# A deformable convolution sampled without gathers: nine taps by dense bilinear weights, on one core of Trainium2

## What is computed

```python
off_out = conv2d(x, off_w) + off_b[None, :, None, None]
o = off_out[:, :2 * DG * K].reshape(Bb, DG, K, 2, Hh, Ww)          # DG = 2 groups, K = 9 taps
mask = jax.nn.sigmoid(off_out[:, 2 * DG * K:]).reshape(Bb, DG, K, Hh, Ww)
py = o[:, :, :, 0] + iy + ky[None, None, :, None, None]
px = o[:, :, :, 1] + ix + kx[None, None, :, None, None]
g = deform_sample(x, py, px) * mask[:, :, None]                    # bilinear, zero outside
out = jnp.einsum('odck,bdckhw->bohw', wr, g)
```

## Time and profile before

| | us |
|---|---|
| three runs | 4657.04, 4685.74, 4686.9 |
| their median | 4685.74 |
| the profiled execution, whole time | 4699.3 |
| its span | 4697.5 |
| mean granted TensorE clock, as a share of 2.4 GHz | 0.774 |

### The profile page before, as it was taken

How to read it: one execution, slowest core, us unless ns; L and a number is a source line. 1 busy time by engine, 2 the same in 40 slices (tenths; PEclk the granted TensorE clock), 3 DMA queues, 4 the chain that set the end, 5 groups by cost and what they waited for, 6 DMA issues and landing times. The chain is left out here.

```text
span 4697.5 us, 54006 instructions
## 1 busy us (share of the span) xinstructions
PE 3017.8 (64%) x20519; PEld 1314.3 (28%) x20519; DVE 2951.6 (63%) x3460; ACT 2245.1 (48%) x1945; POOL 1156.9 (25%) x1229
## 2 busy tenths in 40 slices
PE   3777479999999989999999985143143114411112
PEld 2454333233333333333333332021121112211111
DVE  5999747999999967999999961033321322232222
ACT  1444226999999967999999940000000000000000
POOL 2000010000000000000000002655665665556663
PEclk7665579999999999999999987575566556655555
DMA  2200000000000000000000001112112211211111
GB/s 42 85 1 1 1 3 1 2 1 1 1 2 1 2 1 1 1 1 1 1 2 1 2 13 36 43 42 55 45 49 51 54 47 45 59 40 45 49 44 33
DMA packets 125704, 106.26 MB, mean 23 GB/s; under 512 B 100432, under 2 KB 102608, under 8 KB 125436
## 3 DMA queue, kind: packets, MB, share of 16 engines
q0 software_dynamic: 36864, 75.57, 5.7%
q1 hardware_dynamic: 86940, 26.43, 2.6%
q10 hardware_dynamic: 1632, 0.56, 0.1%
HBM read 82.50 MB, written 19.96 MB: 22 GB/s over the span
## 5 line engine op out<-in xcount | busy, mean ns | idle before, releaser
L1533 ACT ACTIVATE adder_layer_Z<-adder_layer_CP,AN 128x2048 f32 x984 | 1873.9, 2033 | 31.7 <-PE PS L1498 30.9
L1498 PE MATMUL PS<-adder_layer_Z,c_adder_out 128*32 128x512 f32 x16896 | 1843.8, 593 | 57.9 <-ACT adder_layer_Z L1533 33.6
L1579 DVE TENSOR_SCALAR adder_layer_Z<-adder_layer_CP,AW 128x2048 f32 x1128 | 1369.9, 1283 | 43.7 <-PE PS L1498 29.9
L1902 POOL DMA_INDIRECT sampler_G<-neighbours,sampler_IDX x1152 | 1096.5, 952 | 753.5 <-issue 348.3
L1498 PEld LDWEIGHTS PS<-adder_layer_Z,c_adder_out 128*32 128x32 f32 x16896 | 644.5, 110 | 1256.9 <-issue 1187.4
L2038 ACT ACTIVATE sampler_VT<-PS 128x512 f32<-128x512 f32 x64 | 38.2, 598 | 1497.0 <-remote 921.8
L2020 PE MATMUL PS<-sampler_VT,DC 128*64 128x128 f32 (+1 forms) x640 | 157.4, 414 | 897.4 <-ACTq L2041 454.0
L1954 DVE TENSOR_TENSOR sampler_G<-sampler_G,PS 128x2304 f32<-128x2304 f32 x64 | 163.5, 2554 | 840.4 <-issue 436.0
L1586 DVE SCALAR_TENSOR_TENSOR adder_layer_Z<-adder_layer_CP,AW,adder_layer_Z 128x1024 f32<-128x1024 f32 x384 | 476.4, 1282 | 35.6 <-issue 35.6
L2020 PEld LDWEIGHTS PS<-sampler_VT,DC 128*64 128x64 f32 (+1 forms) x640 | 112.9, 210 | 945.5 <-issue 476.0
L2012 PE MATMUL PS<-c_ident,sampler_VAL 128*128 128x128 f32 (+1 forms) x320 | 78.3, 401 | 386.1 <-DVEq L1960 297.3
(11 more groups left out here) (342 smaller groups left out, 2082.4 us busy)
## 6 DMA issues: line engine op xcount, KB each, us to landing
sampler_G<-neighbours,sampler_IDX POOLq DMA_INDIRECT x1152
neighbours<-top_k_zero SPq DMA_DIRECT2D x16, 578.0 KB, 7.2
neighbours<-sampler_HT SPq DMA_DIRECT2D x256, 32.0 KB, 1.7
X<-in_x SPq DMA_DIRECT2D x8, 256.0 KB, 6.2
out<-X SPq DMA_DIRECT2D x8, 256.0 KB, 3.1
P<-in_L_conv_conv_w SPq DMA_DIRECT2D x4, 144.0 KB
P<-in_L_conv_add_w SPq DMA_DIRECT2D x4, 144.0 KB
RAW<-in_L_conv_w SPq DMA_DIRECT2D x4, 144.0 KB
```

Of the source, the lines that this page charges most:

```text
L1498: mm = t.matmul(PS[32 * j:32 * j + 32, k, :], K["adder_out"][:, 32 * i:32 * i + 32], Z[:, r % SLOTS, j, c:c + BANK], start=False, stop=Fal ...
L1533: op = a.activation(z(r, j), seen(ch, ty, tx), ACT.Relu, bias=ANf[:, weight(ty, tx, j, i)])
L1579: op = v.tensor_scalar(z(r, j), seen(ch, ty, taps[0]), AWf[:, weight(ty, taps[0], j, i)], 0.0, ALU.subtract, ALU.max)
L1902: g.indirect_dma_start(G[th % RING][:, k, :], None, tables[b], bass.IndirectOffsetOnAxis(ap=IDX[:, b % 2, step, k:k + 1], axis=0))\
```

## The change

The tables in DRAM, their clearing in an earlier phase (`zero`, 16 transfers of 578 KB), the indices, the gathers and the transposes of sampled values go. In their place each bilinear sample is a dense product: with positions py and px, the value is the sum over all 32 rows y and 32 columns x of relu(1 - |py - y|) * relu(1 - |px - x|) * mask * feature(y, x). Such a function of distance is called a hat.

A quad q is one pair, one half of its pixels (512) and one tap: 4 * 2 * 9 = 72 quads. For a quad, 4 groups (2 halves of the batch by 2 channel groups) take 32 partitions each:
- `positions`: TensorE copies the four groups' py and px from `OFF` to 32 partitions each (8 products); ScalarE makes the hats in two passes (Abs, then Relu).
- `masks`: 4 products copy the mask; VectorE multiplies the x hats by it (`HXM`).
- `spread_x`: 4 products spread the x hats to 128 partitions (4 rows by 32 columns), and ScalarE copies them to `HXS`.
- for each of 8 tiles c of 4 image rows: `spread_y` spreads the y hats of the four groups by 4 products of 32 rows each, in two pairs of PSUM banks; the product with `HXS` (128 x 1024 for each pair) is made by VectorE from PSUM for 10 of the quad's 16 pairs, and for the 6 in `POOLED` by GpSimd, after a copy to SBUF by ScalarE (`move`); `contract` multiplies the features `HT` by these weights with 4 products of 32 columns each, three tiles late (`LAG`).
- ScalarE copies the quad's sums to `V`; after 9 quads `deform` multiplies by the deformable weights (9 products), and the leaky ReLU, the 1x1 convolution and the sum follow as before.

The six banks of PSUM used for spreading are three sets of two (`SETS`), given round in the order of `ring_tiles`: TensorE fills the set of tile n only when tile n - 3 has been read (`await_read`). Bank 6 takes the contraction and bank 7 the convolutions. The stages of the next pair are now halves of 512 pixels, 12 of them, and `background` sets one product of them after each tile c: 100 products in 144 places a pair. SyncE loads five constant tables, and writes the output in halves.

```diff
-TP = H + 2
-NENT = TP * TP
 TILES = PX // 128
-STEPS = TILES * HALVES
-GK = DG * TAPS
+GROUPS4 = HALVES * DG
+QUADS = 2 * NB * TAPS
+SETS = 3
+LAG = 3
+NW = 8
+NE = 3
+POOLED = ((0, 1), (2, 0), (3, 1), (4, 0), (6, 0), (7, 1))
...
+def ring_tiles():
+    tiles = [("pos", 0), ("mask", 0), ("hx", 0, 0), ("hx", 0, 1)]
+    for q in range(QUADS):
+        for c in range(TILES):
+            tiles += [("prod", q, c, 0), ("prod", q, c, 1)]
+            if q + 1 < QUADS:
+                tiles += {1: [("pos", q + 1)], 3: [("mask", q + 1)], 5: [("hx", q + 1, 0)],
+                          6: [("hx", q + 1, 1)]}.get(c, [])
+            if q and q % TAPS == 0:
+                tiles += {4: [("dc", q // TAPS - 1)], 7: [("cv", q // TAPS - 1)]}.get(c, [])
+    return tiles + [("dc", 2 * NB - 1), ("cv", 2 * NB - 1)]
...
+            STAGES = [(s, k) for s in range(6) for k in range(2)]
+            SLOT = 12
+            ws = ("rb_w1", "rb_w2", "off_w", "dc_w")
+            MISC, SUM = 7, 6
+            W = sb("W", [128, NW, 2, BANK])
+            E = sb("E", [128, NE, 2, BANK])
+            HXS = sb("HXS", [128, 2, 2, 2, BANK])
+            HATS = sb("HATS", [128, 2, 2, BANK])
+            HXM = sb("HXM", [128, BANK])
+            V = sb("V", [128, TAPS, BANK])
+            Y = sb("Y", [128, BANK])
+            OFF = sb("OFF", [128, 3, BANK])
+            HT = sb("HT", [128, 2, TILES, 128])
...
+            def ring(n):
+                return PS[:, 2 * (n % SETS):2 * (n % SETS) + 2, :]
...
+            def column(ch):
+                return K["ident"][:, ch:ch + 1].broadcast_to([128, 32])
+            def await_read(engine, n):
+                if n >= SETS:
+                    engine.wait_ge(dve_read if by_dve[n - SETS] else act_read, turn_of[n - SETS])
...
+            def background(q, c):
+                r = TILES * (q % (2 * TAPS)) + c
+                return q // (2 * TAPS) + 1, r // SLOT, r % SLOT
...
                 def _(g):
...
-                    for th in range(NB * STEPS):
-                        b, step = th // STEPS, th % STEPS
-                        if step == 0:
-                            g.wait_ge(indexed, b + 1)
-                            g.wait_ge(stored[b], 16 * NSTORE)
-                        if th >= RING:
-                            g.wait_ge(used, th - RING + 1)
-                        for k in range(GK):
-                            g.indirect_dma_start(G[th % RING][:, k, :], None, tables[b],
-                                                 bass.IndirectOffsetOnAxis(ap=IDX[:, b % 2, step, k:k + 1], axis=0))\
-                             .then_inc(arrived[th % RING], 16)
+                    for j, (_, q, c, pair) in enumerate(shared):
+                        g.wait_ge(act_read, turn_of[number["prod", q, c, pair]])
+                        if TILES * q + c >= NW // 2:
+                            g.wait_ge(summed, TILES * q + c - NW // 2 + 1)
+                        g.tensor_tensor(W[:, slot(q, c, pair)], E[:, j % NE], HXS[:, q % 2, pair], ALU.mult)\
+                         .then_inc(pooled, 1)
...
+                    def product(q, c, pair):
+                        tile = "prod", q, c, pair
+                        if tile in share:
+                            return
+                        n = number[tile]
+                        v.wait_ge(act_read, turn_of[number["hx", q, pair]])
+                        if TILES * q + c >= NW // 2:
+                            v.wait_ge(summed, TILES * q + c - NW // 2 + 1)
+                        v.wait_ge(filled, n + 1)
+                        v.tensor_tensor(W[:, slot(q, c, pair)], ring(n), HXS[:, q % 2, pair], ALU.mult)\
+                         .then_inc(dve_read, 1)
+                    def masks(q):
+                        n = number["mask", q]
+                        v.wait_ge(hats, q + 1)
+                        v.wait_ge(filled, n + 1)
+                        v.tensor_tensor(HXM[:, :], HATS[:, q % 2, 1], ring(n)[:, 0], ALU.mult).then_inc(dve_read, 1)
                 @blk.tensor
                 def _(t):
...
+                    def positions(q):
+                        n = number["pos", q]
+                        b, k, tap = place(q)
+                        await_read(t, n)
+                        t.wait_ge(off_sb, 2 * b + k + 1)
+                        for axis in range(2):
+                            for e in range(GROUPS4):
+                                mm = t.matmul(ring(n)[32 * e:32 * e + 32, axis, :],
+                                              column(64 * (e // DG) + 2 * (e % DG * TAPS + tap) + axis),
+                                              OFF[:, (2 * b + k) % 3], start=True, stop=True)
+                        mm.then_inc(filled, 1)
+                    def masks(q):
+                        n = number["mask", q]
+                        b, k, tap = place(q)
+                        await_read(t, n)
+                        t.wait_ge(sig, 2 * b + k + 1)
+                        for e in range(GROUPS4):
+                            mm = t.matmul(ring(n)[32 * e:32 * e + 32, 0, :],
+                                          column(64 * (e // DG) + 2 * DG * TAPS + e % DG * TAPS + tap),
+                                          SIG[:, (2 * b + k) % 3], start=True, stop=True)
+                        mm.then_inc(filled, 1)
+                    def spread_x(q, pair):
+                        n = number["hx", q, pair]
+                        await_read(t, n)
+                        t.wait_ge(dve_read, turn_of[number["mask", q]])
+                        for i in range(2):
+                            r = 32 * (2 * pair + i)
+                            mm = t.matmul(ring(n)[:, i, :], GR["spread"][r:r + 32, :], HXM[r:r + 32, :],
+                                          start=True, stop=True)
+                        mm.then_inc(filled, 1)
+                    def spread_y(q, c, pair):
+                        n = number["prod", q, c, pair]
+                        await_read(t, n)
+                        t.wait_ge(hats, q + 1)
+                        for i in range(2):
+                            r = 32 * (2 * pair + i)
+                            mm = t.matmul(ring(n)[:, i, :], GR["rows"][r:r + 32, 128 * c:128 * c + 128],
+                                          HATS[r:r + 32, q % 2, 0, :], start=True, stop=True)
+                        mm.then_inc(filled, 1)
+                    def contract(m):
+                        q, c = m // TILES, m % TILES
+                        b = place(q)[0]
+                        for pair in range(2):
+                            await_product(t, ("prod", q, c, pair))
+                        if c == 0:
+                            t.wait_ge(v_sb, q)
+                            t.wait_ge(h_t, 2 * b + 2)
+                        for e in range(GROUPS4):
+                            mm = t.matmul(PS[32 * e:32 * e + 32, SUM, :], HT[:, b % 2, c, 32 * e:32 * e + 32],
+                                          W[:, slot(q, c, e // 2), e % 2, :], start=(c == 0), stop=(c == TILES - 1),
+                                          skip_group_check=True)
+                        mm.then_inc(summed, 1)
...
+                            spread_y(q, c, 0)
+                            spread_y(q, c, 1)
+                            if q + 1 < QUADS:
+                                if c == 1:
+                                    positions(q + 1)
+                                elif c == 3:
+                                    masks(q + 1)
+                                elif c in (5, 6):
+                                    spread_x(q + 1, c - 5)
+                            if q and q % TAPS == 0 and c == 4:
+                                deform(q // TAPS - 1)
+                            if q and q % TAPS == 0 and c == 7:
+                                last_conv(q // TAPS - 1)
+                            b, i, j = background(q, c)
+                            if b < NB:
+                                stage_pe(t, b, i, j)
+                            m = TILES * q + c - LAG
+                            if m >= 0:
+                                contract(m)
...
                 @blk.scalar
                 def _(a):
...
+                    def positions(q):
+                        n = number["pos", q]
+                        a.wait_ge(filled, n + 1)
+                        a.activation(DIST[:, :, :], ring(n), ACT.Abs, bias=GR["hat"][:, 0:1]).then_inc(act_read, 1)
+                        a.drain()
+                        a.activation(HATS[:, q % 2], DIST[:, :, :], ACT.Relu, scale=-1.0, bias=1.0).then_inc(hats, 1)
+                    def spread_x(q, pair):
+                        n = number["hx", q, pair]
+                        if q >= 2:
+                            await_product(a, ("prod", q - 2, TILES - 1, 0))
+                            await_product(a, ("prod", q - 2, TILES - 1, 1))
+                        a.wait_ge(filled, n + 1)
```

(10 more changed lines are left out.)

589 lines of the change are left out of this document (269 added, 320 removed).

## The result

The changed kernel takes 4860.76 us in the median of 4 runs (4857.67 to 4864.26), the kernel before 4686.32 us (4657.04 to 4687.32, 4 runs): 1.0389 times as long, 95% interval 1.036 to 1.0417. Slower was forecast, and the range held it, but at 4760 us the forecast was 101 us low. The profiled span is 4855.9 us. First the page of the changed kernel: the busy time, the line of the granted clock, and the groups by line (busy, mean ns of one | idle time before them and what ended it).

The account below looks back on a forecast made before the run. TensorE was to bound the new sampling: 1725 us of work, 92 of waits and 47 of stages gave 1864; with start 2885 and end 23, 4772 us of span, forecast 4760 against 4685.74 us, range 4600 to 5050.

Parts of the forecast that it names:

- TensorE sets the pace: In the sampling, TensorE at 19.7 us a quad and more was to exceed GpSimd's 18.1, VectorE's 13.0 and ScalarE's 10.9.
- A product 0.86 us, four strips at once: TensorE's f32 product of 512 columns takes 0.86 us; the four strips of a fill run together, also 0.86 us.
- rival 3: In spread_y's fill four strips stream slower than two, 1.23 times the streaming: 1.06 us a fill, 4845 us; chance 0.10.
- 4: In spread_y's fill the two pairs don't overlap at all: 495 us more, less 92 of waits, 5160 us; chance 0.06.
- A change of shape 0.10 us, 1452 of them: TensorE switching between array shapes in the sampling costs 0.10 us each time, bounds 0 and 0.20; 1152 + 300 changes.
- Rival 1: A change of TensorE's array shape costs nothing: -145 us, of which waits take back about 27, 4640 us; chance 0.15.
- Waits for sets, VectorE's stages, the ends, 139 us: TensorE waiting for PSUM sets 92 us, for VectorE's image half stages 32, for ScalarE's stages and ends of halves 15.
- Rival 2: In the sampling, waits for sets and VectorE's stages don't reach TensorE: -139 us, 4620 us; chance 0.12.
- VectorE 1.23 us, ScalarE 1.01, GpSimd 3.0: Sampling: VectorE's product of 1024 columns 1.23 us, a ScalarE copy 1.01 us, a GpSimd product of 1024 columns 3.0 us.
- Rival 5: GpSimd's products bound the sampling: 4800 us at 3.98 us each, 5245 us at 5.43, deciding from 3.6 up; chance 0.07.
- A quad of 21.8 and 25.5 us: One quad of the sampling takes about 21.8 us without image work and 25.5 us with it.
- What bounds the kernel before: In the kernel before, issue of gathers on GpSimd takes 1454 of the sampling's 1803 us; VectorE's idle 840.4 us mirrors it.

Follow-up runs that it names:

- pair_images: Changed kernel with the image products of the background work made two at every second tile step instead of one at each: 4875.17 us.

## Why the prediction was right or wrong

- *TensorE sets the pace:* right. It is busy 96 to 100% of each window at clock 0.98 to 1.00; the large waits of the others are for it, GpSimd's by way of ScalarE's copies. Busy does not mean four strips throughout: in the late fills two run.
- *A product 0.86 us, four strips at once (rival 3 and 4):* right. Where the set of pair 1 is free in time (407 of 576 fills) the records of L2026 start in fours, 0.53 and 0.54 us apart; in the other fills they come in twos because pair 1 waits for its set, which is the wait that was forecast and not a rate. The 0.20 us left over in the earlier trace rows was no rate: it is the change and the longer first round, and with it rival 3's 1.23 falls. A round of four strips takes the 0.43 us of one record in the earlier trace rows, so four strips are four times one. "TensorE: Matmul & The Clock Gate", Part 3, of the Trainium skill states 3.07 times; this trace does not agree.
- *A change of shape 0.10 us, 1452 of them:* **this is the step that failed**. The change is 0.11 us; the term that belongs to it, the first round behind it at f32 weights, was left out. 147 us were forecast for both, 264 us measured (166 for the changes, 98 for the first rounds), and this alone is more than the 95 us that the sampling missed. The upper bound was written down (0.20 us, from the earlier trace rows) and is what a fill of this kind really costs; I took the adder's 0.11 us, where the weights behind the change have 32 columns, for both directions. Rival 1 falls with it. The Trainium skill, "TensorEngine Tiling (Array Packing)", "Key Properties", says that changing the mode drains TensorE and gives no time; the traces show a cost of 0.11 us at each change.
- *Waits for sets, VectorE's stages, the ends, 139 us:* 133 us, right in sum and in mechanism: sets of banks that come late. Inside it the mix differed, and that it adds up is in part luck: no low clock was forecast, and up to 22 us of it came; the waits for sets and VectorE are some 105 us, 41 of them idle time and the rest late fills. The 0.07 us for a load in the 1.55 us of the set's return stood on no row; the loads of L2026 are recorded at 184 ns. Rival 2 falls.
- *VectorE 1.23 us, ScalarE 1.01, GpSimd 3.0:* measured 1.22, 1.02, and 2.36 us. For GpSimd the estimate of 2.25 us from the Trainium skill, "GPSIMD Engine Reference", section 3.1, was nearer. Rival 5 falls; its point of decision was never near.
- *Start 2885, end 23:* 2874 and 22.8.
- *A quad of 21.8 and 25.5 us:* 23.4 us in the last 18 quads and 28.5 us in the first 54, the products of `deform` included. (By its own terms the second figure should have been 25.2.)
- *What bounds the kernel before:* VectorE's 840.4 us ahead of L1954 were read as waiting for the gathers. Their row names issue and ScalarE, and the gathers' data with 42 us only; the reading fits the faster chip (873.4 us for the data), not the one that the forecast was made for. The forecast takes nothing from it, since all of that sampling goes.
- *All in all:* 11 us early, 95 us more, 0 at the end: 84 us on the span. The rest of the 101 us is the 13.6 us that I took off because the profiled run of before lay above its median, where the changed kernel's lay 3 us below (4857.67 of 4860.76).

## What to carry over

A kernel that alternates between ways of splitting TensorE's array pays at each change 0.11 us and, where the weights behind it are f32 with 128 columns, 0.10 us more: count changes as products, at a quarter of a 512-column f32 product. Use bf16 weights where they are exact and the other operand can be split. And once TensorE is full, the cover that its work gives to its readers is part of the design: shortening TensorE's step by 0.52 us gave back only 144 of 300 us, and 258 us once VectorE's bursts were cut up and GpSimd's load was halved; a long wait also costs the clock behind it. Such waits need not show as idle time: look at when the strips start.

## What the runs showed of the hardware

- A VectorE operation with two inputs in SBUF (L1941, 128x512) went from 0.68 to 2.88 us (median) beside GpSimd's products; the products that read PSUM kept their 1.22 us. Giving GpSimd none of the products cost 6.5 us of 4861, in one run.
- TensorE counts as busy with two of four strips running: 155 fills of the changed kernel took 63 us more than the others without a wait in the profile.
- The same kernel with gathers took 4364 us on some chips and 4680 us on others, on the faster ones for want of a wait that the profile does not name. The dense kernel took 4860 to 4862 us in three medians, all on the second kind; its last 18 quads took the same on both kinds (420.6 us, and 420.5 us in pair_images).
